# Down-projection weights rounded with their f32 sums on TensorE, and step sizes made one chunk ahead on VectorE

## What is computed

```python
x = x + attn(bi_wkv(x, fside, fside, w1, u1, cond), w_qkv, w_o)      # 16 heads of 32, causal softmax
x = x + ffn(bi_wkv(x, fside, fside, w2, u2, cond), w_gate, w_up, w_down)
# bi_wkv: sigmoid(r) * (num / den), two decaying sums over the positions, forward and backward
# ffn: inter = silu(q_act(y) @ q_w(w_gate).T) * (q_act(y) @ q_w(w_up).T);  q_act(inter) @ q_w(w_down).T
def _quantize_mx(x, ebits, mfrac, emax_elem, max_norm):   # blocks of 32 along the last axis
    scale = 2 ** (floor(log2(blockmax)) - emax_elem)
    priv = max(floor(log2(|x / scale|)), min_exp)
    q = clip(round(x / scale / 2 ** (priv - mfrac)) * 2 ** (priv - mfrac), -max_norm, max_norm)
    return q * scale
```

## Time and profile before

| | |
|---|---|
| median of 3 runs | 918.21 us (915.83 to 919.13) |
| the profiled execution | 914.99 us |
| its span | 913.2 us |
| mean granted TensorE clock | 0.934 of full |
| busy: TensorE, VectorE, ScalarE | 83%, 85%, 52% |

### The profile page before, as it was taken

How to read it: one execution, slowest core, us unless ns; L and a number is a source line. 1 busy time by engine, 2 the same in 40 slices (tenths; PEclk the granted TensorE clock), 3 DMA queues, 4 the chain that set the end, 5 groups by cost and what they waited for, 6 DMA issues and landing times.

```text
span 913.2 us, 10845 instructions
## 1 busy us (share of the span) xinstructions
PE 759.0 (83%) x3985; PEld 391.3 (43%) x3985; DVE 772.7 (85%) x1122; ACT 471.0 (52%) x710; POOL 73.8 (8%) x149
## 2 busy tenths in 40 slices
PE   4666649298889899897998999978989998999595
PEld 1222224144444344454543444544434445554483
DVE  4999999999997879889988799799887896543887
ACT  4965655358575361476653623766545325453350
POOL 1000001011100002111000021110000120200000
PEclk9676769699999999999899999999999999999798
DMA  9622211256300003754000037540000084500001
GB/s 337 256 76 90 104 57 47 57 126 163 81 23 13 1 12 93 196 150 116 13 24 1 11 73 216 151 104 24 17 7 13 15 207 113 128 1 1 1 1 46
DMA packets 30820, 72.27 MB, mean 79 GB/s; under 512 B 5808, under 2 KB 6832, under 8 KB 28976
## 3 DMA queue, kind: packets, MB, share of 16 engines
q1 hardware_dynamic: 19584, 46.67, 17.1%
q0 software_dynamic: 6144, 16.79, 7.8%
q10 hardware_dynamic: 5040, 8.14, 2.7%
HBM read 33.82 MB, written 4.19 MB: 42 GB/s over the span
## 4 chain that ended last, share of the span: by engine, by line
PE 42%; DVE 34%; issue 8%; ACT 6%; DMA 6%; SPq 3%; POOL 1%; ACTq 0%; DVEq 0%
PE bank L1499 9%; DMA stacks<-rows 5%; PE bank L1394 5%; PE bank L1306 5%; PE bank L1511 5%; PE bank L1365 3%; PE bank L1383 3%; DVE negmax L1029 3%; SPq L318 3%; PE bank L1410 2%; PE bank L1367 2%; PE bank L1332 2%; ACT region L530 2%; DVE fn L909 2%; PE bank L1298 2%
## 5 line engine op out<-in xcount | busy, mean ns | idle before, releaser
L1029 DVE TENSOR_REDUCE negmax<-bank 128x4 f32<-128x512 f32 (+2 forms) x96 | 98.7, 1035 | 39.1 <-PE bank L1339 20.6
L1365 PE MATMUL bank<-stacks 128*128 128x512 f32 (+3 forms) x256 | 106.0, 420 | 28.9 <-ACT region L530 21.0
L530 ACT ACTIVATE region<-bank 128x384 f32<-128x384 f32 (+1 forms) x192 | 95.7, 524 | 63.1 <-PE bank L1368 60.4
L318 POOL DMA_DIRECT2D stacks<-rows x128 | 69.8, 553 | 721.0 <-DVE region L806 350.2
L1306 PE MATMUL bank<-h,wqkv 128*128 128x512 f32 x256 | 115.2, 601 | 4.2 <-DVE region L1259 4.2
L1332 PE MATMUL bank<-stacks 128*128 128x128 f32 (+3 forms) x256 | 79.8, 406 | 7.2 <-DMA stacks<-rows 4.8
L1367 PE MATMUL bank<-maxrow,pick 128*128 128x512 bf16 (+3 forms) x256 | 82.9, 324 | 0.0
L1365 PEld LDWEIGHTS bank<-stacks 128*128 128x128 f32 x256 | 51.8, 202 | 59.0 <-ACT region L530 38.5
L1306 PEld LDWEIGHTS bank<-h,wqkv 128*128 128x128 f32 x256 | 48.4, 193 | 61.5 <-issue 55.4
L1298 PE MATMUL bank<-wqkv,h 128*128 128x512 f32 x128 | 60.9, 620 | 4.7 <-DVE h L957 4.7
L1552 PE MATMUL bank<-region,ident 128*128 128x512 f32 x64 | 49.0, 926 | 11.9 <-DVE identb L860 11.9
(11 more groups left out here) (178 smaller groups left out, 1485.6 us busy)
## 6 DMA issues: line engine op xcount, KB each, us to landing
stacks<-rows SPq DMA_DIRECT2D x128, 128.0 KB, 4.1
stacks<-rows POOLq DMA_DIRECT2D x128, 128.0 KB, 4.7
kt<-in_fside ACTq DMA_DIRECT2D x30, 256.0 KB, 3.3
region<-in_w_gate SPq DMA_DIRECT2D x4, 1024.0 KB, 11.3
h<-in_x SPq DMA_DIRECT2D x4, 1024.0 KB, 5.6
xt<-in_x SPq DMA_DIRECT2D x4, 1024.0 KB, 7.8
region<-in_w_up SPq DMA_DIRECT2D x4, 1024.0 KB, 6.2
region<-in_w_down SPq DMA_DIRECT2D x4, 1024.0 KB, 4.7
```

The costliest lines, as they stand in the source:

```text
L318: eng.dma_start(stacks[HD * r:HD * r + HD, at:at + 2, i, :].bitcast(F32), rows[mine, q:k + 1:k - q, :]).then_inc(stacked[s][i], 16)
L530: nc.scalar.activation(probs[:, i, P_AT[tiles[0]]:P_AT[tiles[0]] + columns], bank[4 + n % 2][:, 0:columns], ACT.Exp, scale=SCALE).then_inc ...
L1029: nc.vector.tensor_reduce(o, scored, AX_X, ALU.max, negate=True).then_inc(max_taken, 1)
L1365: nc.tensor.matmul(o, ks[s][:, i, P * t:P * t + P], qs[s][:, i, P * t:T], start=True, stop=False, skip_group_check=True)
```

## The change

The down chunks are summed like the others, by TensorE, but in banks 0 to 3. `down_to_round(n)` copies a chunk's weights there by an f32 product with the identity once the steps of the chunk before have been read (`quartered`) and the scales stand; `add_down_rounding(n)` adds the bf16 steps. The four pairs are set among the projections of batch 0. VectorE drops its sum L839, and makes the step sizes of chunk n + 1 ahead of the rounding of chunk n. ScalarE's `whole_steps` reads the banks. TensorE waits for the last chunk's `whole_steps` before `turn(0)`, which uses banks 0 to 3.

```diff
@@ whole_steps (ScalarE)
-                sums = banks[:, 4:8, :] if n < 2 * WC else landing(2 * WC + ROUNDING[n - 2 * WC])
+                sums = banks[:, 4:8, :] if n < 2 * WC else banks[:, 0:4, :]
@@ VectorE
-        def sum_weights(ch, n, scales, src, mag):
+        def magnitude_steps(ch, n, scales, mag):
 
             ch.link(nc.vector.tensor_scalar(mag.bitcast(U16), mag.bitcast(U16), 0x7F80, None, ALU.bitwise_and))
             ch.eng.wait_ge(scaled, 3 * scales + 1)
             nc.vector.tensor_tensor(mag, mag, over(scale_b), ALU.max).then_inc(stepped, 1)
-            if n >= 2 * WC:
-                ch.eng.wait_ge(stepped, n + 1)
-                nc.vector.scalar_tensor_tensor(src, mag, ROUND_1_BIT, src, ALU.mult, ALU.add).then_inc(summed_w, 1)
@@ VectorE, the down chunks
+            magnitude_steps(ch, first, first, rounded(first + ROUNDING[0]))
             for k, c in enumerate(ROUNDING):
-                sum_weights(ch, first + k, first, landing(first + c), rounded(first + c))
                 if k == 0:
                     backward(-1, 9, 0)
                     backward(-1, 9, 1)
...
                 else:
                     finish(-1, 9)
+                if k + 1 < FC:
+                    magnitude_steps(ch, first + k + 1, first, rounded(first + ROUNDING[k + 1]))
                 round_weights(ch, first + k, first, rounded(first + c))
@@ TensorE
+            def down_to_round(n):
+
+                pe.wait_ge(scaled, 3 * (2 * WC + 1))
+                pe.wait_ge(quartered, n)
+                for j in range(CJ):
+                    nc.tensor.matmul(bank[j][:, :], ident[:, :], landing(2 * WC + ROUNDING[n - 2 * WC])[:, j, :], start=True, stop=False)
+
+            def add_down_rounding(n):
+
+                pe.wait_ge(stepped, n + 1)
+                for j in range(CJ):
+                    mm = nc.tensor.matmul(bank[j][:, :], round_ident[:, :], rounded(2 * WC + ROUNDING[n - 2 * WC])[:, j, :],
+                                          start=False, stop=True)
+                mm.then_inc(summed_w, 1)
@@ TensorE, its program between the block scales and turn(0)
             spread_tops(2 * WC)
+            down_to_round(2 * WC)
+            add_down_rounding(2 * WC)
             for s in range(2):
                 project_qk(0, 0, s)
+            down_to_round(2 * WC + 1)
             for s in range(2):
                 leave_low(0, 0, s)
+            add_down_rounding(2 * WC + 1)
             pe.wait_ge(v_copied, 2)
             for s in range(2):
                 project_qk(0, 1, s)
+            down_to_round(2 * WC + 2)
+            add_down_rounding(2 * WC + 2)
             pe.wait_ge(qk_low, 2)
             for s in range(2):
                 project_qk(0, 3, s)
-            pe.wait_ge(scaled, 3 * (2 * WC + 1))
+            down_to_round(2 * WC + 3)
+            add_down_rounding(2 * WC + 3)
+            pe.wait_ge(quartered, 2 * WC + FC)
```

More of the change, by code:

```diff
@@ L969, in _ @@
                     top_magnitude(ch, n + 1, True)
-                sum_weights(ch, n, n, landing(n), rounded(n))
+                magnitude_steps(ch, n, n, rounded(n))
                 if n == 0:
```

## The result

The changed kernel takes 926.81 us (median of 4 runs, 925.8 to 929.5) against 917.42 us before: a ratio of 1.0107, 95% interval 1.0077 to 1.0137, so 9.4 us slower. The forecast was 5.8 us. The profiled execution is the slowest of the four, 929.5 us; that of before, 914.99 us, lies under all four timed ones. Their difference of 14.5 us must not be read as the effect.

The account below looks back on a forecast made before the run. VectorE was taken to bound the down chunks; with the change TensorE would, ending the last steps 6.1 us later, less 0.3 for `leave_low`: 918.21 + 5.8 = 924.0 us, 8 in 10 for 918.5 to 928.5.

Parts of the forecast that it names:

- VectorE sets the pace, 8.8 us leave it: Down chunks of the kernel before: VectorE is the bound there, and dropping four sums takes 8.8 us from it.
- TensorE's course: Down chunks: TensorE works without idle time from 138.8 to 180.6 us, with 17.2 us of added work.
- Last steps 6.1 us later: End of the down chunks: the last `whole_steps` ends at 182.5 us in place of 176.4.
- VectorE's waits of 2.4, 5.1, 2.0, 5.4: Down chunks: VectorE's four idle times, in us, ahead of the products, released by ScalarE and behind it TensorE.
- `leave_low` at half clock: Ahead of the first turn: after a 3.6 us pause TensorE runs two matmuls at half clock, 0.3 us less than before.
- The kept clock: Rival, chance 0.20: pause too short for a clock fall, or an earlier first rise; 4.4 or 4.0 us slower, 922.3 us.
- Making step sizes ahead saves nothing by itself: Down chunks: it lets TensorE find them ready and only moves 2 us of VectorE's work into its wait.
- One to one into the total: From the last `whole_steps` through all four turns: any shift there shows fully in the total, 5.8 us.
- the main case: Whole kernel, chance 0.53: TensorE sets the down chunks' pace, two matmuls after them at half clock; 924.0 us, range 921 to 927.

Follow-up runs that it names:

- delay: Kernel before, with eight unread VectorE products of 512 f32 elements ahead of the last down chunk's sum; 923.31 us, ratio 1.0050.
- steps_ahead: Kernel before, with VectorE making step sizes and its own sum of chunk n + 1 ahead of the rounding of chunk n; 914.43 us, ratio 0.9969.
- filler: Changed kernel, with two more unread VectorE products of 512 f32 elements per down chunk, between step sizes and rounding; 926.43 us, ratio 1.0108.
- no_copies: Changed kernel without the f32 copies of the down weights to banks 0 to 3, so its sums hold the steps alone; 916.57 us, ratio 0.9984.
- more_code: Kernel before, with 50 unread TensorE products of 16 columns (100 instructions) in its idle time ahead of the first turn; 920.35 us, ratio 1.0033.
- again: The changed kernel measured once more, word for word; 924.06 us, ratio 1.0068 to the kernel before.
- the eight: The eight measurements of kernels with more TensorE instructions than the kernel before; seven lose 2 to 5 us in the turns, mean 3.0 us.
- two_aligned: Changed kernel with only chunks 9 and 11 summed on TensorE, plus 103 products of 16 columns at TensorE's start; 907.53 us, ratio 0.9901.
- two_again: Changed kernel with only chunks 9 and 11 summed on TensorE, 8 and 10 on VectorE, step sizes ahead; second measurement, 912.92 us, ratio 0.9967.
- three_on_pe: Changed kernel with chunks 9, 10 and 11 summed on TensorE, 8 on VectorE, last chunk's pieces between the last projection's halves; 918.19 us, ratio 1.0002.

## Why the prediction was right, and where it was off

- **VectorE sets the pace, 8.8 us leave it.** Right for the kernel before: its one wait was of 0.17 us, and delay shows the first turn hanging on that stretch. More exactly, as steps_ahead shows, the turn hangs on the last `whole_steps` and so on what VectorE does ahead of it.
- **TensorE's course.** Right in each step: `down_to_round(8)` took 5.46 us (reckoned 5.4), each later copy 3.43 from start to start (3.4), the bf16 products 0.87 (0.9), the end at 180.0 (180.6). It had no idle time. filler and no_copies show that this and not VectorE's length is what counts.
- **Last steps 6.1 us later.** Measured 5.6 by the clock of the span, 5.9 from the first step sizes, and 4.9 from TensorE's first copy of weights (12.57 us, before 11.91).
- **VectorE's waits of 2.4, 5.1, 2.0, 5.4.** Measured 2.51, 5.35, 2.05, 5.30.
- **`leave_low` at half clock.** TensorE paused 3.60 us, and the two took 3.35 us (3.55 before): the granted clock was full until 183.0 and half from then (0.52 in 183.00 to 183.50), so it fell in the pause, 0.6 us before the first of them. The kept clock was the rival; it didn't come true here.
- **Making step sizes ahead saves nothing by itself.** The prediction says this of the changed kernel, where TensorE's length would hide a gain; no run tests it there, and it wasn't a term of the sum. It must not be carried to VectorE's own sums: in steps_ahead, with each sum beside its step sizes, it gains 2 to 3 us, because the last `whole_steps` comes earlier.
- **One to one into the total.** This is the step that was mis-sized: "any shift of that moment I expect in the total one to one, since all four turns follow it". delay agrees for a shift, or is a little below (6.6 us at the first maxima, 4.7 at the end), but the sum left out a term, the cost of TensorE's some 100 more instructions in the turns: +3.5 us in more_code. 5.8 + 3.5 = 9.3, against measured 9.4, 5.4 (again) and, with the filler, 9.1. The 3.0 on average over the eight is no independent check, since these three are among them.
- **The time.** 926.81 us lies inside the 918.5 to 928.5 forecast, and even in the 921 to 927 of the main case. That is in part luck: 3 to 4 of the 9.4 us come from a term that the range wasn't made for, and found room in the margin for clock and scatter.

Shown is that TensorE's longer work makes the stretch late, and that 50 small products in TensorE's idle time cost about 3 us (1.6 to 4.5 by the interval of the ratio) with nothing late. Shown too is that filling at the start gives it back, and more: two_aligned against two_again leaves no doubt (0.9901 against 0.9967, intervals apart), while for the changed kernel 1.0031 is clear of 1.0107 but its interval overlaps that of 1.0068. That it must be 256 instructions isn't shown, because filling of another size wasn't run. That the delay comes from the load of code on q8 among the stacks' transfers is read from the traces and not shown by taking the load away; how one 16 KB load would hold them up for 1 to 2 us stays open, so does the part of the clock, and so does why filled kernels beat the kernel before in the turns.

## What to carry to other kernels

Before work moves from a full engine to one with free time, lay the new work along that engine's own order, with the clock that it will have and with what stands ahead and behind: 16.7 free us didn't take 17.2 of work that also began later and partly at half clock, while half of the work fitted and was faster. Move as much as makes both equally long and try each share. When a change adds instructions to a long program, compare it with a version that has the same number of idle ones; here that made 3 us.

## What the runs showed of the hardware that wasn't expected

- 50 products of 16 columns in idle time, which nobody waits for, made the kernel 0.33% slower (1.0017 to 1.0049).
- The same kind of filling at the start, sized to 256 instructions in all, made the half change 5.4 us faster than without it in the same set (907.53 against 912.92), though the filling took TensorE under 3 us of idle time and the first maxima came no earlier (176.92 against 176.83).
- One kernel's executions scatter by 10 us (914.82 to 925.13 in 29 runs of the kernel before), more than most of the effects here. The granted clock goes with it: 0.921, the lowest of the 29, in the slowest of them, and in the twelve of three_on_pe 0.941 to 0.943 in the four fastest (911.5 to 914.1 us) and 0.929 to 0.933 in the three slowest (921.8 to 923.8).
